# Deformable stage: GpSimd's products of hats are gated on points of VectorE's program

## What is computed

```
out = relu(group_norm(conv1x1(x, w1)))            # 1024 -> 256
om  = conv3x3(out, w_off) + b_off                 # 27 channels
off_x, off_y, mask = om[:, :9], om[:, 9:18], sigmoid(om[:, 18:])
sampled = bilinear_sample(out, grid_y + off_y, grid_x + off_x) * mask
out = relu(group_norm(einsum(sampled, w2)))       # 9 taps, 256 -> 256
out = relu(group_norm(conv1x1(out, w3)) + x)      # 256 -> 1024
```

## Time and profile before

| | us |
|---|---|
| median of 3 runs | 2977.31 (2972.14 to 2982.18) |
| the profiled execution, its own time | 2978.64 |
| its span, first to last instruction | 2976.6 |
| TensorE matmuls busy | 2915.8 (98%) |
| VectorE busy | 2397.4 (81%) |
| ScalarE busy | 1795.9 (60%) |
| GpSimd busy | 712.0 (24%) |

### The profile page before, as it was taken

The page is one execution under the profiler, slowest core; times in us unless marked ns, Lnnn a source line. Parts: engine busy times, 40 slices in busy tenths (PEclk is TensorE's granted clock), DMA queues, the critical chain, the costliest instruction groups (busy, mean ns, idle before and its releaser), DMA issues.

```text
span 2976.6 us, 46528 instructions
## 1 busy us (share of the span) xinstructions
PE 2915.8 (98%) x16518; PEld 2864.6 (96%) x16518; DVE 2397.4 (81%) x4872; ACT 1795.9 (60%) x3281; POOL 712.0 (24%) x433
## 2 busy tenths in 40 slices
PE   9999999999998999999999999999999999999997
PEld 9999999999997899999999999999999999999997
DVE  5655888965666688898888988888888888889885
ACT  5544322346664566676666666676776667666664
POOL 0000000000001333333333333333333333333331
PEclk9999999999999999999999999999999999999998
DMA  7774111035653344444444444544444444454431
GB/s 270 218 234 131 44 44 44 22 128 201 262 225 114 122 151 154 152 144 153 152 154 151 143 156 145 163 147 146 159 145 162 146 147 156 149 158 149 147 119 73
DMA packets 209207, 437.39 MB, mean 147 GB/s; under 512 B 18640, under 2 KB 170192, under 8 KB 203344
## 3 DMA queue, kind: packets, MB, share of 16 engines
q1 hardware_dynamic: 159408, 326.82, 32.6%
q10 hardware_dynamic: 49568, 107.60, 11.1%
HBM read 307.71 MB, written 126.64 MB: 146 GB/s over the span
## 4 chain that ended last, share of the span: by engine, by line
PE 56%; DVE 10%; ACT 1%; issue 0%; DMA 0%; POOL 0%; ACTq 0%; SPq 0%; DVEq 0%; POOLq 0%
PE sample L86 6%; PE sample L91 6%; PE deform L86 6%; PE deform L91 6%; PE sample L87 6%; PE deform L87 6%; PE work L86 5%; PE work L91 5%; PE work L87 5%; DVE s_lo L1805 3%; DVE x L1829 2%; DVE x L1711 1%; DVE x_lo L1717 1%; DVE v_lo L1813 1%; PE work L73 1%; PE work L75 1%
## 5 line engine op out<-in xcount | busy, mean ns | idle before, releaser
L1667 POOL TENSOR_TENSOR hats<-hats 98x784 f32<-98x784 f32 x288 | 597.6, 2075 | 909.8 <-DMA hats<-hat_scratch 888.9
L1459 ACT ACTIVATE v_hi<-sample 128x392 fp32r<-128x392 f32 (+1 forms) x640 | 292.2, 463 | 322.5 <-PE sample L91 312.7
L86 PE MATMUL sample<-s_hi,aT_hi 98*128 98x392 f32 (+1 forms) x1280 | 418.1, 332 | 6.4 <-DVE v_lo L1813 6.1
L87 PE MATMUL sample<-s_hi,aT_lo 98*128 98x392 f32 (+1 forms) x1280 | 412.7, 328 | 0.0
L86 PE MATMUL deform<-v_hi,w_w 128*128 128x392 f32 x1152 | 403.7, 350 | 0.0
L87 PE MATMUL deform<-v_hi,w_w 128*128 128x392 f32 x1152 | 393.2, 341 | 0.0
L1813 DVE TENSOR_TENSOR v_lo<-sample,v_hi 128x392 fp32r<-128x392 f32 (+1 forms) x640 | 326.4, 517 | 71.1 <-ACT v_hi L1459 69.9
L1805 DVE TENSOR_TENSOR s_lo<-hats,s_hi 98x784 fp32r<-98x784 f32 x288 | 360.1, 1251 | 2.7 <-ACT s_hi L1450 1.7
L91 PE MATMUL sample<-s_lo,aT_hi 98*128 98x392 f32 (+1 forms) x1280 | 316.4, 328 | 7.1 <-DVE s_lo L1805 7.1
L91 PE MATMUL deform<-v_lo,w_w 128*128 128x392 f32 x1152 | 310.7, 342 | 0.0
L1450 ACT ACTIVATE s_hi<-hats 98x784 fp32r<-98x784 f32 x288 | 245.5, 853 | 105.6 <-DVE x L1711 78.3
(11 more groups left out here) (226 smaller groups left out, 7254.5 us busy)
## 6 DMA issues: line engine op xcount, KB each, us to landing
hats<-hat_scratch SPq DMA_DIRECT2D x768, 150.1 KB
x<-in_x SPq DMA_DIRECT2D x64, 784.0 KB, 5.9
in_home<-y_scratch ACTq DMA_DIRECT2D x248, 196.0 KB, 3.1
out<-x ACTq DMA_DIRECT2D x62, 784.0 KB, 3.4
y_home<-in_x SPq DMA_DIRECT2D x32, 784.0 KB, 4.9
y_scratch<-y_out SPq DMA_DIRECT2D x16, 1568.0 KB, 5.9
terms<-in_x SPq DMA_DIRECT2D x30, 784.0 KB, 4.6
y_scratch<-y_home SPq DMA_DIRECT2D x15, 1568.0 KB, 5.1
```

Of the source, the lines that this page charges most:

```text
L86: nc.tensor.matmul(out, w_hi, x_hi, start=start, stop=False)
L87: nc.tensor.matmul(out, w_lo, x_hi, start=False, stop=False)
L1459: nc.scalar.activation(v_hi[:, group % 2, c, 0:taps_of(g), i, :], sample[:, t % 2, 0:cols(g)].rearrange("p (k s) -> p k s", s=PIX), ACT.Co ...
L1667: nc.gpsimd.tensor_tensor(hats[:, slot, 0:2, 0:n], hats[:, slot, 0:2, 0:n], hats[:, slot, 2:3, 0:n].broadcast_to([HALF, 2, n]), ALU.mult). ...
```

## The change

On GpSimd, `make_s` gets a second wait: for units 2, 3, 5, 6 and 8 on `s_lo` of the unit before (`s_lo_made`), for unit 4 on `b_lo` of the pair before (`b_lo_made`). Units 0, 1 and 7 keep the wait on their loads alone. Product 5 moves in the program from the end of one iteration to behind the root of gn1 in the next, and the root of gn2 to ahead of product 4. On VectorE, `add_y(after, 3)` moves to the front of the step, `rest_v(before, 18)` ahead of `rest_x1(after, 1)`, `rest_s(now, 1)` ahead of `rest_aT(now, 1)`, `rest_s(now, 2)` ahead of `rest_v(now, 2)`, `count_b` ahead of `rest_v(now, 3)`, and `rest_s(now, 7)` ahead of `count_y(before, 6)`.

```diff
@@ make_s, GpSimd
                 pool.wait_ge(hats_loaded[slot], 48 * (unit // HATS + 1 + (p.n + u // (UNITS - 1) if slot == HATS - 1 else 0)))
+
+
+                if u in (2, 3, 5, 6, 8):
+                    pool.wait_ge(s_lo_made, unit)
+                elif u == 4:
+                    at_least(pool, b_lo_made, p.n)
                 nc.gpsimd.tensor_tensor(hats[:, slot, 0:2, 0:n], hats[:, slot, 0:2, 0:n],
@@ step, GpSimd
                 root(now, gn1)
+                make_s(before, 5)
                 make_s(before, 6)
...
                 make_s(now, 3)
+                root(before, gn2)
                 make_s(now, 4)
-                root(before, gn2)
-                make_s(now, 5)
@@ step, VectorE
+                add_y(after, 3)
                 rest_v(before, 16)
                 rest_aT(now, 0)
                 rest_v(before, 17)
-                add_y(after, 3)
+                rest_v(before, 18)
                 rest_x1(after, 1)
                 rest_s(now, 0)
-                rest_v(before, 18)
                 rest_v(before, 19)
                 add_x1(past, 5)
                 rest_x1(after, 2)
                 add_y(after, 4)
+                rest_s(now, 1)
                 rest_aT(now, 1)
-                rest_s(now, 1)
...
+                rest_s(now, 2)
                 rest_v(now, 2)
-                rest_s(now, 2)
+                count_b(before)
                 rest_v(now, 3)
-                count_b(before)
...
                 rest_v(now, 10)
+                rest_s(now, 7)
                 count_y(before, 6)
-                rest_s(now, 7)
                 count_y(before, 7)
                 reduce_y(before)
```

## The result

The changed kernel is slower. Its median is 3000.12 us (five runs, 2997.57 to 3004.19) against 2978.58 us for the kernel before in the same comparison (five runs, 2972.14 to 2982.18). The ratio is 1.0076, with a 95% interval of 1.0062 to 1.0091. The profiled execution of the changed kernel took 3004.01 us, its span 3001.8 us, the granted clock was 0.994 in both. The forecast was 2961 and its range ended at 2979; the first rival, the lost race at the end of product 8, had 2993.

The account below looks back on a forecast made before the run. TensorE was taken to set the pace, with 0.87 us a period above 61.46 lost to a late VectorE. Less 0.21 and 0.10, 0.56 a period, 16.2 us in 29, gave 2961 us, range 2952 to 2979.

Parts of the forecast that it names:

- the first rival: End of product 8: the mask's product starts before L1124 and stalls VectorE's squares and sums; 2993 us, chance 0.18.
- The step that failed: Unit 8: product 8 ends later, L1124 still precedes the mask's product, tile 13 starts 0.21 us a period later.
- The rival's own working: Unit 8, race lost: mask's product ends at 2621.5, tile 13 starts at 2622.55, 1.3 us behind the quick period's.
- 61.46: A period as quick as any, in us, TensorE busy throughout; the change could give back nothing below it.
- the steps on units 2 to 6: Units 2, 3: `s_lo` wait gone, 0.1 us a period cost; unit 4 hides in 0.45 us; units 5, 6 nothing.
- One sign of being wrong: ScalarE's `s_hi` waiting for products, listed among what would show the forecast wrong.
- the 0.1 us taken for a late `v_lo` of tile 3: TensorE's tile 5, behind product 3: `v_lo` of tile 3 late, between nothing and 0.3 us, taken as 0.1 a period.
- A second step failed: `add_y(3)` ahead of tiles 16 and 17: 0.6 us if its load is late, otherwise clear of product 1; taken as nothing.
- The second rival: New waits, `v_lo` of tile 3 0.3 to 0.6 us late or `s_hi` held: 2966 to 2976 us, chance 0.22.

Follow-up runs that it names:

- e3: The changed kernel with GpSimd's mask product also waiting for the sum behind the third GroupNorm's squares (L1124): 2959.61 us, ratio 0.9950.
- e1: The changed kernel with `add_y(after, 3)` back at its old place behind `rest_v(before, 17)`: 2978.74 us, ratio 1.0014.
- e4: The changed kernel with `add_y(after, 3)` back and the mask's product waiting for the sum (L1124): 2956.56 us, ratio 0.9942.
- e9: The kernel before with only `s_lo` of unit 7 moved ahead of `count_y(before, 6)`, no gate: 2994.93 us, ratio 1.0066.
- e5: The changed kernel with `add_y(after, 3)` back and the mask's product ahead of product 8, no wait added: 2950.41 us, ratio 0.9902.
- e8: The kernel before with one gate, product 3 waiting for `s_lo` of unit 2: 2966.44 us, ratio 0.9956.

## Why the prediction was wrong

**The step that failed** is unit 8, in the sentence that the mask's product "starts at once" and yet that L1124 "gets in" before it, for 0.21 us a period. It took the 0.20 us between the two GpSimd instructions of the earlier trace rows for the time from one to the next. They were ScalarE's signal: the mask had become ready only 0.05 us after the product's end. Where the mask has long been ready the interval is -0.04 us by the record, and L1124, which starts 0.09 to 0.1 us after the end, comes second every time (in the one place of 30 without it, L1121 does). The prediction named this, with that very doubt about, as its first rival; the argument against it, that a semaphore is looked at between the two, rested on a start behind a signal, which isn't the case at hand. Tile 13 starts 0.75 us later in the kernel after than in e3 (1.78 against 1.03 us behind product 8's end). The means say the same: 62.51 in e1 less 61.77 in e4 is 0.74. The rival's own working had 1.3 less 0.21, so 1.09: it let L1680 start 0.07 us behind the product where it starts 0.04 before its end, and took 1.03 us from L1680's end to the tile from a place where L1121 was the held one, where behind a held L1124 it is 0.80 (2073.99 to 2074.79). These two make up the 0.34 us.

**The sum was right without that step.** e3, the changed kernel with only this race decided the other way, has 61.89 us a period, where the prediction's terms give 61.77 (61.46, 0.21 and 0.10), and took 2959.61 us against 2961; e4, which has `add_y(3)` back as well, has 61.77 and took 2956.56. L1835 stays under 0.5 us, `s_lo` of unit 2 takes 0.96, TensorE waits for no `s_lo`, and product 4 ends 0.53 us or more ahead of `s_hi` in all pairs but the first and the last: the steps on units 2 to 6 held. One sign of being wrong did show, at no cost: ScalarE's `s_hi` of unit 2 begins 0.03 us behind its product in nearly every pair, so it waits for it, but never by more than 0.15 us in the 29 periods. TensorE's slack at tile 5 was 0.73 us in the mean, so the 0.1 us taken for a late `v_lo` of tile 3 was somewhat too much.

**A second step failed**: `add_y(3)` at the front, costed at nothing, in a range from nothing to 0.6. The 0.6 was its own length without a stall, taken on the ground that it left product 1's way. It didn't: the load lands 6.45 us in the mean behind the pair's first transpose, and product 1 starts at 6.60, so the two meet and the bound should have been the stalled length, 2.14 us. That costs 17.3 us from start to start, 21.4 by e1. But it needs the lost race. Product 1 starts 7.21 us behind the transpose in the kernel before and 7.61 in e3, where the waits at tile 18 are few or none. That a lost race makes it earlier shows inside the trace of the kernel before: 6.35 in the mean in the 7 periods that follow one, 7.48 in the 22 others. In e9, where one edit makes the race lost, it is 6.37. The reason, that TensorE is held at tile 13 while the mask, and the load of hats that follows it, is not, is argued, and no run tests it. This second loss is why the result lies 7 us above the first rival's 2993, although the race by itself cost less than it said (62.51 us a period in e1, against 62.86).

**The chances.** The cases were the right ones, and the weights were not. The mechanism that I priced from one precedent had 0.18, and by the evidence at hand it turned on whether one interval was a wait; with no other row of that kind, the two sides stood nearer to even. One row of another kind stood in the trace of the kernel before, unread. In the first layer ten memsets of GpSimd (L709, L710) follow one another with nothing between them, and each of the last nine starts 0.057 to 0.067 us before the recorded end of the one ahead:

```profile
287.43 0.26 POOL L710 MEMSET w_w<- 128x192 f32 x1
287.63 0.26 POOL L709 MEMSET point_lo<- 128x192 f32 x1
```

They have no semaphore to wait for between them, so they don't settle it, but they speak for the rival.

The second rival's new waits at tile 5 hardly came: three in e3, 1.1 us in all.

The Trainium skill ("SBUF — State Buffer", Who interferes with whom) has it that GpSimd and VectorE share a pair of ports as an exclusive lock, and that whoever issues first gets it for the whole instruction. The trace agrees: L1124 is held to the end of L1680 (0.94 us), L1149 to the end of product 8 (1.62 us) in e5. It doesn't fit the one L1121 of 2.38 us, which was issued before L1680 and still came behind it. The prediction said that by this rule all hung on the 0.1 us at product 8's end, and for the race so it was.

## What to carry to other kernels

An instruction that shares a port should be placed by what stands next on the other engine and who waits for it, and not only moved off what it stalls now: the gate of product 8 laid it beside statistics, which a product never stalls, and put its end on the two small sums that TensorE waits for. Where two instructions stand back to back on the holding engine, count them as one block for whatever comes after the first has ended; in the changed kernel with `add_y(3)` back (e1), holding the short one behind the critical sums brought 22 us (e4), and running it ahead of the long one 28 (e5), while the one gate tried alone brought 11 (e8). And an interval taken from a precedent is good only if the precedent waited for the same thing.

## What was unexpected of the hardware

- GpSimd's next instruction, when its inputs are ready, is recorded as starting 0.032 to 0.064 us before the end of the one ahead, in 30 of 30 places of the kernel after; an instruction of VectorE that comes 0.1 us after that end stands behind both. An instruction already held by the first (L1121) finishes between the two in 29 of the 30, by the record 0.06 us after the first's end; in the one left it stood behind both, 2.38 us.
- The length of the held instruction doesn't matter: 128x32 (0.20 us alone) took 0.94, and 128x2 (0.16 alone) took 1.62.
- The load of `in_home` for `add_y(3)`, issued on ScalarE's queue, took some 5.2 us in the mean to land in the kernel after, where the median of all such loads is 3.4.

At which moment the port changes hands stays open; the records show only starts and ends.
